# Half of the last layer's token batches prepared ahead of the expert loop, the other half inside its first steps, with row copies behind the first scattered pairs

## The reference, cut to what matters

```python
flat = hidden_states.reshape(-1, d)                     # 4096 tokens, d = 128
probs = jax.nn.softmax(flat @ gate_W.T, axis=-1)        # 8 experts
top_v, top_i = jax.lax.top_k(probs, 2)
g = silu(flat @ w1_e);  u = flat @ w3_e;  out_e = (g * u) @ w2_e     # F = 512
routed = sum over the two chosen experts of top_v * out_e
gs = silu(flat @ w1_s); us = flat @ w3_s; shared = (gs * us) @ w2_s / 8
return 0.5 * shared + 0.5 * routed
```

## Time and profile before

| | us |
|---|---|
| three runs, median | 1882.97 |
| lowest and highest | 1881.5 and 1886.79 |
| profiled execution, its own time | 1877.83 |
| profiled execution, span from first to last instruction | 1876.1 |
| PE busy in the span | 1531.1 (82%) |
| DVE busy | 1278.9 (68%) |
| ACT busy | 1024.1 (55%) |
| POOL busy | 786.3 (42%) |

### The profile page before, as it was taken

The page is one execution under the profiler, slowest core; times in us unless marked ns, Lnnn a source line. Parts: engine busy times, 40 slices in busy tenths (PEclk is TensorE's granted clock), DMA queues, the critical chain, the costliest instruction groups (busy, mean ns, idle before and its releaser), DMA issues. The chain is left out here.

```text
span 1876.1 us, 26759 instructions
## 1 busy us (share of the span) xinstructions
PE 1531.1 (82%) x8752; PEld 970.7 (52%) x8757; DVE 1278.9 (68%) x3228; ACT 1024.1 (55%) x1747; POOL 786.3 (42%) x902
## 2 busy tenths in 40 slices
PE   4788787279999999677459999999998585999990
PEld 2444554247666666443125555555553574777770
DVE  2557656367777777466758877778883483788875
ACT  2345544315666665534425767677766553677762
POOL 2133333344555554324751112221100377488875
PEclk8899898658999999978867999999999598999995
DMA  7600000132222221000053544444430011444425
GB/s 215 229 1 1 1 1 1 38 98 71 71 71 71 71 72 42 3 12 1 1 127 99 129 126 117 119 104 113 120 89 2 24 61 55 139 136 120 134 59 135
DMA packets 96202, 144.30 MB, mean 77 GB/s; under 512 B 31267, under 2 KB 59940, under 8 KB 91953
## 3 DMA queue, kind: packets, MB, share of 16 engines
q1 hardware_dynamic: 91072, 134.11, 25.8%
q0 software_dynamic: 4992, 8.48, 1.4%
HBM read 104.19 MB, written 57.48 MB: 86 GB/s over the span
## 5 line engine op out<-in xcount | busy, mean ns | idle before, releaser
L1193 DVE TENSOR_REDUCE ctx_nm<-ctx_s 128x1 f32<-128x512 f32 x512 | 329.4, 681 | 95.5 <-PE ctx_s L1469 94.6
L1305 ACT ACTIVATE ctx_probs<-ctx_st 128x1024 f32<-128x1024 f32 x256 | 254.0, 1022 | 113.4 <-PE ctx_st L1485 109.0
L1193 DVE TENSOR_REDUCE rope_nm<-rope_s 128x1 f32<-128x128 f32 (+3 forms) x512 | 230.2, 481 | 86.1 <-PE rope_s L1472 84.0
L1305 ACT ACTIVATE rope_probs<-rope_st 128x1024 f32<-128x1024 f32 (+1 forms) x256 | 172.2, 702 | 138.5 <-PE rope_st L1485 137.3
L1469 PE MATMUL ctx_s<-ctx_kst,ctx_qst 96*128 96x512 f32 x512 | 220.0, 467 | 17.3 <-DMA ctx_kst<-ctx_contexts 8.4
L1469 PE MATMUL rope_s<-rope_kst,rope_qst 96*128 96x128 f32 (+3 forms) x512 | 185.2, 395 | 4.0 <-DVE rope_nm L1193 3.2
L1058 POOL TENSOR_SCALAR_AFFINE_SELECT rope_probs<-rope_probs 128x256 f32<-128x256 f32 x256 | 98.3, 409 | 170.0 <-ACT rope_probs L1305 169.5
L1469 PEld LDWEIGHTS ctx_s<-ctx_kst,ctx_qst 96*128 96x128 f32 x512 | 100.0, 196 | 131.2 <-DVE ctx_nm L1193 54.9
L1485 PE MATMUL ctx_st<-ctx_qst,ctx_kst 98*128 98x512 f32 x512 | 164.5, 404 | 2.4 <-ACT ctx_probs L1305 2.4
L1485 PE MATMUL rope_st<-rope_qst,rope_kst 98*128 98x512 f32 (+3 forms) x512 | 141.0, 359 | 3.9 <-ACT rope_probs L1305 3.9
L2665 DVE TENSOR_TENSOR sw_hl<-sw_hf,sw_hh 128x512 fp32r<-128x512 f32 x124 | 129.9, 1047 | 0.1
(11 more groups left out here) (382 smaller groups left out, 3354.3 us busy)
## 6 DMA issues: line engine op xcount, KB each, us to landing
sw_raw<-in_L_ffn_all SPq DMA_DIRECT2D x24, 768.0 KB, 4.5
sw_xs<-in_pad SPq DMA_DIRECT2D x65, 260.0 KB, 9.8
rope_halves<-rope_qk SPq DMA_DIRECT2D x24, 512.0 KB, 4.7
ctx_halves<-ctx_qk SPq DMA_DIRECT2D x24, 512.0 KB, 6.2
ctx_qst<-ctx_contexts SPq DMA_DIRECT2D x32, 384.0 KB
ctx_kst<-ctx_contexts SPq DMA_DIRECT2D x32, 384.0 KB
rope_qst<-rope_halves SPq DMA_DIRECT2D x32, 192.0 KB
rope_kst<-rope_halves SPq DMA_DIRECT2D x32, 192.0 KB
```

The lines of the kernel that those rows point to most:

```text
L1193: nc.vector.tensor_reduce(nm[:, g, j * T + t:j * T + t + 1], bank("s", b, n)[:, 0:keys], AXX, ALU.max, negate=True).then_inc(s_used, 1)
L1305: nc.scalar.activation(probs[n // GH % 2][:, n % GH, u * units[0]:u * units[0] + units[u]], st_bank[u][:, 0:units[u]], ACT.Exp, scale=SCAL ...
```

## The change

Only batches 0 to 3 (EARLY = 4) go through the front ahead of the loop. The transposes, `keep`, scores, normalising and moments of the batches 4 to 7 are issued in the first steps of the expert loop (batch 4's moments, offsets and `normalise`, and batch 5's moments, stay ahead of it). The late batches share one PSUM bank (`t_out`) for their transposes, and their logits lie in `t_in` instead of a `d` bank. `token_high(0)` and `token_low(0)` move forward into the front, `cut_high(0)` and `cut_low(0)` go to other places in it. The copies of the batches 5, 6 and 7 stand on POOL behind the first, second and third scattered pair, and `rsqrt(7)` behind the first. `shift(1)` and `exponent(1)` move into step 7 and `gate(1)` starts in step 8; `ranks(1)`, `place(1)` and `plan` move from step 8 to step 13. The pairs' wait on `hf_ready` becomes `pace(n)`: 2 for n = 0, and 27 for n = 31.

```diff
+        EARLY = B // G
+        flips = g_bank + u_bank + [t_out] * EARLY
+        logits = [d_bank[0][:, 0:GN * NE], t_in[:, 256:256 + GN * NE]]
...
-        LATER, PER_STEP = 8, 2
+        RANKS, SHIFT, LATER, PER_STEP = 1, 7, 13, 2
+        pace = lambda n: RANKS + 1 + 13 * n // 16
...
@@ PE @@
             def turn(b):
                 pe.wait_ge(y_ready, b + 1)
-                if b >= 4:
-                    pe.wait_ge(yT_ready, b - 3)
+                if b > EARLY:
+                    pe.wait_ge(yT_ready, b)
...
             def score(b):
                 pe.wait_ge(yT_ready, b + 1)
+                if b == EARLY:
+                    pe.wait_ge(slots_ready, 1)
...
-            for b in range(B):
-                if b + 2 < B:
+            for b in range(EARLY):
+                if b + 2 < EARLY:
                     turn(b + 2)
                 score(b)
-            pe.wait_ge(yT_ready, B)
             for m in range(M + LAG):
...
+                if m == 0:
+                    turn(EARLY)
+                if m == RANKS:
                     ranks(0)
+                if 2 <= m < 2 + EARLY - 1:
+                    turn(EARLY + m - 1)
+                if 3 <= m < 3 + EARLY:
+                    score(EARLY + m - 3)
                 if m == LATER:
                     ranks(1)
...
@@ ACT @@
-            for b in range(B):
+            for b in range(EARLY):
                 keep(b)
-                if b + 2 < B:
+                if b == 0:
+                    token_high(0)
+                if b + 2 <= EARLY:
                     normalise(b + 2)
-                if b == 3:
+                if b == 1:
                     cut_high(0)
-                if b == 6:
-                    exponent(0)
-            exponent(1)
-            token_high(0)
+            exponent(0)
             for m in range(M):
                 i, c = m // FC, m % FC
                 gated(m)
                 if m >= 1:
                     high_half(m - 1)
+                if m == 1:
+                    keep(EARLY)
+                if 3 <= m < EARLY + 2:
+                    keep(EARLY + m - 2)
+                if 1 <= m < EARLY:
+                    normalise(EARLY + m)
+                if m == SHIFT:
+                    exponent(1)
...
@@ POOL @@
             def scatter(g):
...
-                    pool.wait_ge(hf_ready, n + 1)
+                    pool.wait_ge(hf_ready, pace(n))
                     for k in range(2):
...
+                    if EARLY + 1 + n < B:
+                        copy(EARLY + 1 + n)
+                    if EARLY + 3 + n < B:
+                        rsqrt(EARLY + 3 + n)
...
             rsqrt(0)
-            for b in range(B):
-                if b + 1 < B:
-                    rsqrt(b + 1)
+            for b in range(EARLY):
+                rsqrt(b + 1)
                 copy(b)
-                if b == 4:
-                    cut_low(0)
+            cut_low(0)
+            copy(EARLY)
+            rsqrt(EARLY + 1)
+            rsqrt(EARLY + 2)
...
@@ DVE @@
+            input_moments(0)
+            for b in range(EARLY + 1):
+                input_moments(b + 1)
                 offsets(b)
...
-                if b == 5:
-                    shift(0)
+                if b == 2:
+                    token_low(0)
+            shift(0)
             dve.wait_ge(first_loaded, 16 * len(first_loads))
             for _ in gate(0):
                 pass
-            shift(1)
-            token_low(0)
             later = gate(1)
             for m in range(M):
                 i, c = m // FC, m % FC
                 product(m)
-                for _ in range(PER_STEP):
+                for _ in range(PER_STEP if m > SHIFT else 0):
                     next(later, None)
                 if m >= 1:
                     low_half(m - 1)
...
-                if m == 1:
+                if m < EARLY - 1:
+                    if EARLY + 2 + m < B:
+                        input_moments(EARLY + 2 + m)
+                    offsets(EARLY + 1 + m)
+                if m == RANKS:
                     place(0)
+                if m == SHIFT:
+                    shift(1)
```

More of the change, by code:

```diff
@@ L2188, in routed_layer @@
         t_in, t_out = ps("t_in"), ps("t_out")
-        flips = g_bank + u_bank
-        logits = d_bank
+        EARLY = B // G
+        flips = g_bank + u_bank + [t_out] * EARLY
+        logits = [d_bank[0][:, 0:GN * NE], t_in[:, 256:256 + GN * NE]]
         gw, order, tables, marks = sb("gw", [P, NE]), sb("order", [P, NE]), sb("tables", [P, 3, P]), sb("marks", [P, NE + 64 + NT + NE])
@@ L2287, in turn @@
                 pe.wait_ge(y_ready, b + 1)
-                if b >= 4:
-                    pe.wait_ge(yT_ready, b - 3)
+                if b > EARLY:
+                    pe.wait_ge(yT_ready, b)
                 for t in range(T):
-                    last = nc.tensor.transpose(tile(flips[b % 4], t), rows[:, b * T + t, 0, 0:D], ident[:])
+                    last = nc.tensor.transpose(tile(flips[b], t), rows[:, b * T + t, 0, 0:D], ident[:])
                 last.then_inc(flip_ps, 1)
@@ L2339, in down @@
                 if c == 0:
-                    if i < 2:
-                        pe.wait_ge(lg_ready, i + 1)
-                    else:
+                    if i == 0:
+                        pe.wait_ge(lg_ready, 1)
+                    elif i >= 2:
                         pe.wait_ge(dT_ready, i - 1)
@@ L2361, in turn_out @@
                     pe.wait_ge(yo_ready, i)
+                else:
+                    pe.wait_ge(yT_ready, B)
                 for t in range(T):
@@ L2400, in keep @@
                 act.wait_ge(flip_ps, b + 1)
-                nc.scalar.activation(YT[:, b * S:(b + 1) * S], flips[b % 4][:], ACT.Copy).then_inc(yT_ready, 1)
+                nc.scalar.activation(YT[:, b * S:(b + 1) * S], flips[b][:], ACT.Copy).then_inc(yT_ready, 1)
             def cut_high(s):
@@ L2604, in shift @@
                 dve.wait_ge(logit_ps, (g + 1) * B // G)
-                raw_logits = logits[g][:, 0:GN * NE].rearrange("p (n e) -> p n e", e=NE)
+                raw_logits = logits[g].rearrange("p (n e) -> p n e", e=NE)
                 ch.do(nc.vector.tensor_reduce(red[:, part, 0], raw_logits, AXX, ALU.max))
@@ L2690, in residual, with input_moments @@
                 nc.vector.tensor_tensor(x, x, chosen[b][:, :, 1, :], ALU.add).then_inc(done, 1)
[L2692 to L2695, removed]
+            def input_moments(b):
+                moments(b, X[:, b * T:(b + 1) * T, :])
+            input_moments(0)
+            for b in range(EARLY + 1):
+                input_moments(b + 1)
                 offsets(b)
```

## The result

| | before | after |
|---|---|---|
| median of 14 runs | 1882.86 us | 1876.31 us |
| lowest run | 1876.65 us | 1869.62 us |
| profiled execution, own time / span | 1877.83 / 1876.1 us | 1872.82 / 1871.1 us |

The ratio is 0.996, with a 95% interval of 0.9948 to 0.9972: 5.3 to 9.8 us faster. The ratios of this study are not quotients of the two medians, which would give 0.9965 here; the two differ by up to 0.001. One of the 14 runs of after took 5455.28 us; it doesn't move the median. The forecast was 1874.8 us in a range of 1869.5 to 1880.5, and faster as the likeliest sign.

The account below looks back on a forecast made before the run. POOL's fixed-rate line of 64 scatters was taken to set the first routed matmul. Starting 12.8 us earlier, less 4.2 for insertions and 0.4 for busier engines, gains 8.2 us: median 1874.8 us, range 1869.5 to 1880.5.

Parts of the forecast that it names:

- The start of the line: First of POOL's 64 scatters, behind `place(0)`: 12.8 us earlier, at 1492.6 (1491 to 1496).
- What is put into the line: Three copies and one `rsqrt` between POOL's scatters, with their breaks: 4.2 us added, bounds 2.84 and 5.3.
- 0.4 for a busier neighbourhood: Added to POOL's line because a larger part of it runs beside busy engines: 0.4 us.
- the 3 x 0.45 us of hand-over and longer scatter: At POOL's breaks: each costs about 0.14 us of hand-over and a scatter of 1.29 against 0.95; 1.35 us in all.
- The wait of `offsets(7)`: DVE waits for `rsqrt(7)` on POOL, behind the first pair and copy(5): 2 to 4 us of a step.
- The cover: PE's idle time ahead of the first routed tile: some 11 us instead of 21.8, so longer shared tiles cost nothing.
- The pacing: Pairs waiting for `pace(n)` products: tightest at pair 9, at 1520.6, with `product(8)` at 1513.5, 7 us ahead.
- rival (a): PE's clock stays low through the mixed steps and pacing takes over: gain 3.0 us, 1880.0; chance 0.10.
- the forecast's 1.5: Within the time to `product(8)`: low clock on PE at the start of the steps costs 1.5 us.
- (b): The line's start moves less, `place(0)` waiting in order on DVE; first scatter at 1496, gain about 4.5, 1878.5; chance 0.08.
- (c): Shared tiles become the bound, the clock staying low past the mixed steps: 26 us slower, 1909; chance 0.05.
- (d): No gain: breaks and waits in POOL's line eat 12 us; 1883; chance 0.05.

Follow-up runs that it names:

- e_ahead: The changed kernel with copy(5) and `rsqrt(7)` ahead of the first scatter, copy(6) and copy(7) one pair earlier; 1873.18 us, 0.993 of the kernel before.
- e_simple: The kernel before with only `ranks(0)` and `place(0)` moved right behind `gate(0)` and no wait on `hf_ready`; 1924.04 us, 1.0154 of the kernel before.
- e_simple2: e_simple with `exponent(0)` also moved up by two batches and `ranks(0)` behind score(5); 1920.28 us, 1.0133 of the kernel before.
- e_nopace: The changed kernel without pacing, every pair waiting only for 2 products; 1909.69 us, 1.0071 of the kernel before.
- e_rank0: The changed kernel with `ranks(0)`, `place(0)` in step 0, copy(5) ahead of the line, `rsqrt(7)`, copy(6), copy(7) behind pairs one, one, two; 0.9966 of the kernel before.
- e_rank0p: e_rank0 with each pair waiting for one product more; 1892.18 us, 0.9982 of the kernel before.
- e_simple_p: e_simple with the old wait put back, pair n waiting for n + 1 products; 1893.56 us, 0.9987 of the kernel before.

## Why the prediction was right, step by step

| step, us into the layer | forecast | measured |
|---|---|---|
| `gate(0)` starts | 21.0 | 21.20 |
| mask done | 25.8 | 25.98 |
| cast of the counts | 31.2 | 30.62 |
| first scatter | 34.7 | 34.12 |
| product(8), wanted by pair 9 | 55.6, wanted 62.7 | 55.9, pair 9 at 61.06 |
| second group's slots, and their first pair | 75, 81 | 73.4, 79.5 |
| shared tiles end | 117.7 | 116.9 |
| last scatter starts | 122.8 | 120.50 |
| first routed matmul | 131.8 | 129.36 |

(Forecasts less 1457.91, measured less 1464.15.)

**The start of the line, right.** 13.4 us earlier in this pair of profiles and 12.7 in the repeated pair, against 12.8. Half of it comes from fewer batches in front (the mask is 6.8 us earlier), half from what stands between mask and first scatter (8.1 us instead of 14.7).

**What is put into the line, too dear by a third.** The sum had 4.2 us for the breaks and 0.4 for a busier neighbourhood; the line grew by 2.87 us, 83.51 to 86.38 from the first start to the last. The mis-sized term is the 3 x 0.45 us of hand-over and longer scatter. By the rows above, three copies of 0.62 and the `rsqrt` of 1.05 are 2.9; the pauses of 0.20, 0.17 and 0.16 replace three of 0.30, which takes 0.4 off; and the 64 scatters sum to 65.64 us against 65.25, with 17 of them over 1.03 us in both kernels. So longer scatters come anyway, about one in four, and the breaks added none to their number. I had read the one of 1.29 us in the earlier trace rows as the price of a break. The 0.4 rested in part on a slip: of the 14 POOL instructions in the 16.7 us of the earlier trace rows 13 are scatters (the last is the weights' cut behind the line), so a scatter took 1.28 us there and not 1.19, against 1.33 in the busy stretch. The lower bound of the estimate, the bare 2.84, is the measured one, and e_ahead confirms it: with copy(5) and `rsqrt(7)` out of it, the line is 1.7 to 2.0 us shorter, for 1.67 us of work.

**The wait of `offsets(7)`, right.** 2.91 us on POOL's `rsqrt(7)`, forecast 2 to 4, and nothing behind it was late for the line.

**The cover, right in place.** PE's pause ahead of the routed tiles shrank from 21.8 to 9.55 us, forecast 11. The pacing never held the line: of eight waits for a product in POOL's queue the longest is 0.30 us.

**The clock: rival (a) didn't occur.** The mixed steps ran at 1.00 from 1498.3 to 1528; windows of after, the first of them in the front:

```profile
1475.80:1484.00 8.20, 8.20 (x40) 8.20 (x40) 1.95 (x16) 5.83 (x12) 6.60 (x6) 0.50 0.00 0
...
1490.26:1495.11 4.85, 0.21 (x2) 0.04 (x3) 4.66 (x24) 2.76 (x6) 1.01 (x1) 0.62 0.01 2
1495.11:1498.30 3.19, 3.19 (x9) 2.53 (x10) 1.71 (x7) 1.43 (x4) 0.03 (x1) 0.51 0.02 5
1498.30:1510.00 11.70, 9.89 (x59) 8.09 (x57) 5.22 (x10) 7.97 (x18) 10.24 (x11) 1.00 0.10 34
1510.00:1528.00 18.00, 14.76 (x72) 11.62 (x71) 13.16 (x31) 11.16 (x19) 13.74 (x15) 1.00 0.15 49
```

The low level came once near there, when PE stood 4.64 us for the counts, and went after 3.2 us of work, wide matmuls but for its first and last instructions. At half speed that cost 1.6 us, and the forecast's 1.5 was right. The rule of the Trainium skill that spoke for this rival ("TensorE: Matmul & The Clock Gate", part 4, PE-mode transpose), that transposes don't count as busy time like matmuls, is not contradicted: here they stood among wide matmuls. The front agrees with it as before: PE was busy with turns and scores for all 8.20 us from 1475.80 to 1484.00, at 0.50.

**Rivals (b), (c), (d).** The first scatter is not late (b), PE does pause (c), and the breaks are cheap (d). But (c) names a danger that is real in neighbouring kernels: in e_simple, e_simple2 and e_nopace PE goes into the routed tiles without a pause, and they are 13.7 to 29.8 us slower than before. (It does so in e_rank0 and e_rank0p too, which are faster than before, so the sign alone is no proof of a loss.) The way there was another, though: ACT and DVE started late. The granted clock was 0.73 beside e_simple's line, but PE was busy for only 44.59 of those 95.08 us and stood for the rest.

**From the layer to the median.** By the marks the layer gained 11.2 us in this pair of profiles and 8.2 in the repeated one; the medians differ by 6.5 and 9.1. The forecast of 8.2 lies among them, and that is in part luck: in the first pair the first routed matmul came 10.6 us earlier, 2.4 more than forecast, while the median fell by 1.7 less than forecast. What stands between the 11.2 us of the layer and the 6.5 of the median is not shown. The lower end of the range has a slip of 0.2 us: 1882.97 less 10 and 3 is 1870.0, not 1869.8; it decided nothing. The profiled spans alone (5.0 and 1.1 us apart) would have misled, since the layers ahead differ by up to 15 us from execution to execution.

**What stays open.** What makes ACT and DVE start late. That the pace changes its cost rests on two comparisons, neither of them pure: e_simple and e_simple_p differ in the pace alone but ran on two chips, and e_nopace and e_rank0p shared a chip but differ in more. The chip may decide whether it occurs (argued only). Also whether the change gains as much on chips like B and C: the kernel as changed wasn't run there.

## What to carry to other kernels

Where a fixed-rate line of DMA issues sets the end, count only its start and what is put into it. A short instruction in the line cost its own duration here and no more; one that fits into the wait ahead of the line cost nothing, so put it there. Keep a line of indirect DMAs paced by the work beside it, but no tighter than that work's rate: 13/16 of a product per pair made the line 4.3 us shorter than one per pair, and no pace at all lost 13.7 us against the kernel before, on a chip where every kernel profiled had late starts. Compare executions from a mark inside the changed layer, not from the start of the program.

## What the runs showed of the hardware

Beside unpaced scatters, one every 1.27 us, ACT and DVE started instructions late: up to 10.54 us after PE's last work (a SiLU of e_simple) and 7.15 us after the input was there (a product). The scatters themselves kept 0.96 us and 0.30 us of pause. It happened in all six kernels profiled on the chips B and C, the three paced ones of e_simple_p, e_rank0 and e_rank0p among them, and in none of the eight on the others. The Trainium skill, "SBUF — State Buffer", in its warning on DVE and DMAs issued from GpSimd, tells of the opposite direction: DVE holds a port that they share, and the descriptors come late. Nothing here shows that: the scatters kept their rate, and it was ACT and DVE that came late. By the same page GpSimd can hold that port against DVE too, but ACT has ports of its own, so the rule does not explain the late SiLUs.
